# Attention: the outputs' halves turned by transposing DMAs instead of on TensorE, and the fusing products one slot later

## The reference, cut to what matters

```
q    = ln(gelu(x @ Wq @ Wt + bt))                      # 4 groups x 12 heads x 64 = 3072 columns
qf   = concat(relu(q), relu(-q)) / sqrt(128)
out  = (qf @ kv) / (qf @ ksum + 1e-6)                  # per group and head, 64 columns each
h   += gelu(ln(out @ Wf + bf)) @ Wo + bo               # out: [n, 3072], Wf: [3072, 768]
```

## Time and profile before

| | |
|---|---|
| median of 3 runs | 2499.05 us (2498.91 to 2499.41) |
| profiled execution, own time | 2497.05 us |
| its span | 2495.3 us |
| PE, DVE, ACT, POOL busy | 95%, 82%, 74%, 52% of the span |
| mean granted clock of TensorE | 0.984 of full speed |
| attention, about | 706 to 2435 us of the span |
| PE, DVE, ACT, POOL busy of the 200 us from 1200 | 197.5, 161.5, 156.0, 133.2 us |
| idle before the fusing products, on o_lo | 21.7 us, 41 times |
| DMA in attention | none but the loads at its beginning |

### The profile page before, as it was taken

One profiled execution on the slowest core, in us unless ns is written; L12 is line 12 of the kernel. 1 busy time (PEld: TensorE's weight loads), 2 busy tenths in 40 slices (PEclk: granted clock), 3 DMA queues, 4 the chain that ended last, 5 costly groups with the idle time before them and its releaser, 6 DMA issues. The chain is left out here.

```text
span 2495.3 us, 61438 instructions
## 1 busy us (share of the span) xinstructions
PE 2370.7 (95%) x22026; PEld 1669.4 (67%) x22026; DVE 2038.6 (82%) x3219; ACT 1839.3 (74%) x2892; POOL 1292.9 (52%) x1253
## 2 busy tenths in 40 slices
PE   5999999899989999999999999999999999999985
PEld 3777776666656666666666666766666666666654
DVE  7999999878867878787878787878878787878755
ACT  6777777566667777778777878787777778777854
POOL 0000000256666666666666666666666666666660
PEclk9999999999989999999999999999999999999997
DMA  6421111111100000000000000000000000000002
GB/s 142 127 58 38 38 45 31 35 52 44 51 13 2 1 0 0 0 0 0 0 0 0 0 0 0 0 0 0 0 0 0 0 0 0 0 0 0 0 1 64
DMA packets 21800, 46.28 MB, mean 19 GB/s; under 512 B 5684, under 2 KB 12340, under 8 KB 21428
## 3 DMA queue, kind: packets, MB, share of 16 engines
q1 hardware_dynamic: 20596, 45.06, 7.0%
q10 hardware_dynamic: 1152, 0.51, 0.1%
HBM read 41.62 MB, written 3.93 MB: 18 GB/s over the span
## 5 line engine op out<-in xcount | busy, mean ns | idle before, releaser
L1091 ACT ACTIVATE phi<-ps_t,betat,gt 64x512 f32<-64x512 f32 (+1 forms) x1280 | 852.2, 666 | 17.1
L1338 POOL TENSOR_TENSOR phi_lo<-phi 128x512 bf16<-128x512 f32 x480 | 515.4, 1074 | 550.4 <-ACT phi L1091 550.4
L1018 PE MATMUL ps_y<-staging,o_hi 128*128 128x384 bf16 x1920 | 468.7, 326 | 21.7 <-DVE o_lo L1208 21.7
L1018 PE MATMUL ps_y<-staging,o_lo 128*128 128x384 bf16 x1920 | 468.9, 326 | 0.0
L1018 PE MATMUL ps_y<-wf_lo,o_hi 128*128 128x384 bf16 x1920 | 468.9, 326 | 0.0
L1330 POOL TENSOR_TENSOR q_ssq<-q_ssq,half 128x8 f32<-128x8 f32 x240 | 439.2, 1830 | 18.8
L1208 DVE TENSOR_TENSOR o_lo<-ps_u,o_hi 128x512 bf16<-128x512 f32 x240 | 164.4, 685 | 213.9 <-ACT o_hi L1101 213.9
L172 PE MATMUL acc<-w_b,feat 128*128 128x384 bf16 x1728 | 295.5, 331 | 34.2 <-ACT feat L223 28.1
L1101 ACT ACTIVATE o_hi<-ps_u 128x512 bf16<-128x512 f32 x240 | 143.5, 598 | 239.3 <-PE ps_u L1004 239.3
L1018 PEld LDWEIGHTS ps_y<-staging,o_lo 128*128 128x128 bf16 x1920 | 187.9, 98 | 124.2
L1018 PEld LDWEIGHTS ps_y<-wf_lo,o_hi 128*128 128x128 bf16 x1920 | 187.7, 98 | 124.3
(11 more groups left out here) (268 smaller groups left out, 5427.9 us busy)
## 6 DMA issues: line engine op xcount, KB each, us to landing
xt<-in_x_dram SPq DMA_DIRECT2D x32, 320.0 KB, 5.2
ex_big<-in_wf_dram SPq DMA_DIRECT2D x24, 384.0 KB, 3.2
xt<-in_x_dram SPq DMA_DIRECT2D x32, 256.0 KB, 5.7
out_dram<-h SPq DMA_DIRECT2D x8, 480.0 KB, 4.6
staging<-in_wq_t_dram SPq DMA_DIRECT2D x1, 3072.0 KB, 12.6
staging<-in_tok_w_dram SPq DMA_DIRECT2D x8, 240.0 KB, 10.4
staging<-in_tok_w_dram SPq DMA_DIRECT2D x8, 192.0 KB, 10.3
staging<-in_kv_w_dram SPq DMA_DIRECT2D x1, 1536.0 KB, 15.8
```

Source lines behind the costliest of these rows:

```text
L1018: last = nc.tensor.matmul(ps_y[:, n, 0:HC], lhs, w[part][:, c, n * HC:(n + 1) * HC], start=c == 0 and lhs is oh and part == 'wf_hi', stop= ...
L1091: last = nc.scalar.activation(phi[sign * DH:(sign + 1) * DH, j % 2, a:b, head, :], ps_t[rows, a * P:b * P].rearrange("p (i n) -> p i n", n ...
L1338: nc.gpsimd.tensor_tensor(phi_lo[:, j % 2, :, head], phi[:, j % 2, :, head], phi_hi[:, j % 2, :, head], ALU.subtract).then_inc(s["phi_lo_d ...
```

## The change

The halves are now made before the turning. ACT rounds o (in SBUF) into `oh[:, j % 2, 0]`, DVE subtracts into `oh[:, j % 2, 1]`, and SP issues one transposing DMA of the 128 x 1024 bf16 of both into `ot`, with a semaphore for each of the two buffers. PE's `turn_outputs` and the PSUM tile ps_u are gone. `fuse` waits for the DMA and runs in slot k + 3 instead of k + 2. All of the end of a tile moves a slot: `move_y` to slot 3, the root and normalizing to 4, PE's turning and ACT's gelu to 5, `low_ys` and `project_out` to slot 0 of the tile after (the latter still last in PE's slot), `add_to_h` to slot 1, and USES is ordered anew. The last `low_ys` and `project_out` stand behind all slots. In the draining pass GpSimd's `row_roots` stands ahead of `low_ys`. xn, xl and xe move into unused parts of other tiles; one semaphore less is used for the slots' norms.

```diff
-        xn = sb("xn3", [P, 2 * P], F32)
+        xn = flat[:, RING * OC + INNER + OC:]
-        xl = sb("xl3", [P, P], BF16)
-        xe = sb("xe3", [P, P], BF16)
+        xl, xe = (ex['spare'][:, n * P:(n + 1) * P] for n in range(2))
-        o_hi = sb("o_hi", [P, 2, OC], BF16)
-        o_lo = sb("o_lo", [P, 2, OC], BF16)
+        oh = sb("o_halves", [P, 2, 2, OC], BF16)
+        ot = sb("o_turned", [P, 2, 2, PAIRS, P], BF16)
...
-        USES = ("oct3", "oct4", "oct5", "x", "oct0", "oct1", "f0", "f1", "oct2", "r")
+        turned = [sem(f"at_o_turned{n}") for n in range(2)]
+
+        USES = ("oct3", "r", "oct4", "oct5", "x", "oct0", "oct1", "oct2", "f0", "f1")
...
+                def turn_outputs(tile, j):                       # on SP
+                    sp.wait_ge(s["o_lo_done"], count(tile, j, NO))
+                    if (n := earlier(tile, j, NO, 2)) is not None:
+                        sp.wait_ge(s["fused"], n)
+                    sp.dma_start(ot[:, j % 2].rearrange("p k i n -> p (k i) n"),
+                                 oh[:, j % 2].rearrange("p k c -> p (k c)"), transpose=True).then_inc(turned[j % 2], 16)
...
-                def turn_outputs(tile, j):                       # on PE
-                    pe.wait_ge(s["o_done"], count(tile, j, NO))
-                    ...
-                    for i in range(PAIRS):
-                        last = nc.tensor.transpose(ps_u[:, i * P:(i + 1) * P],
-                                                   o[:, i // 2, 2 * (i % 2):2 * (i % 2) + 2].rearrange("p h d -> p (h d)"), ident[:, :])
                 def fuse(tile, j):
-                    pe.wait_ge(s["o_hi_done"], count(tile, j, NO))
-                    pe.wait_ge(s["o_lo_done"], count(tile, j, NO))
+                    pe.wait_ge(turned[j % 2], 16 * count(tile, j // 2, NO // 2))
...
                 def slot(tile, j):                               # on PE
-                    if j == 4 and tile.prev().real:
+                    if j == 5 and tile.prev().real:
                         turn_y(tile.prev(), 0, tile)
...
-                    of, k = octet(tile, j - 2)
+                    of, k = octet(tile, j - 3)
                     if of.real:
                         fuse(of, k)
-                    of, k = octet(tile, j - 1)
-                    if of.real:
-                        turn_outputs(of, k)
-                    if j == 5 and tile.prev().real:
-                        project_out(tile.prev(), tile)
+                    if j == 0 and tile.prev().prev().real:
+                        project_out(tile.prev().prev(), tile)
                 all_slots(pe, slot)
+                project_out(Tile(TILES - 1), Tile(TILES + 1))
...
                 def high_outputs(tile, j):
-                    act.wait_ge(s["o_turned"], count(tile, j, NO))
-                    ...
-                    nc.scalar.activation(o_hi[:, j % 2], ps_u[:, 0:OC], ACT.Copy).then_inc(s["o_hi_done"], 1)
+                    act.wait_ge(s["o_done"], count(tile, j, NO))
+                    if (n := earlier(tile, j // 2, NO // 2, 1)) is not None:
+                        act.wait_ge(turned[j % 2], 16 * n)
+                    nc.scalar.activation(oh[:, j % 2, 0], o[:, :, :, :].rearrange("p a h d -> p (a h d)"),
+                                         ACT.Copy).then_inc(s["o_hi_done"], 1)
...
                 def low_outputs(tile, j):
                     dve.wait_ge(s["o_hi_done"], count(tile, j, NO))
-                    ...
-                    nc.vector.tensor_tensor(o_lo[:, j % 2], ps_u[:, 0:OC], o_hi[:, j % 2],
-                                            ALU.subtract).then_inc(s["o_lo_done"], 1)
+                    nc.vector.tensor_tensor(oh[:, j % 2, 1], o[:, :, :, :].rearrange("p a h d -> p (a h d)"),
+                                            oh[:, j % 2, 0], ALU.subtract).then_inc(s["o_lo_done"], 1)
...
                 def slot(tile, j):                               # on GpSimd
                     if j == 0 and not tile.real and tile.prev().real:
                         row_roots()
-                    if j == 3 and tile.prev().real:
+                    if j == 4 and tile.prev().real:
                         rstd_y(tile.prev())
-                    if j == 5 and tile.prev().real:
-                        low_ys(tile.prev())
+                    if j == 0 and tile.prev().prev().real:
+                        low_ys(tile.prev().prev())
...
                 all_slots(pool, slot)
+                low_ys(Tile(TILES - 1))
```

More of the change, by code:

```diff
@@ L750, in expert_tiles @@
         at += size
+    ex['spare'] = big[:, at:].bitcast(BF16)
     return ex
@@ L899, in read_after @@
                 return tile.next(), [("xe_ready", 0, 1), ("xl_ready", 0, 1)]
-            return tile.prev(), [("h_part", 0, 1)] if use == "r" else [("ys_done", int(use[1:]), 2)]
+            if use == "r":
+                return tile.prev().prev(), [("h_part", 0, 1)]
+            return tile.prev(), [("ys_done", int(use[1:]), 2)]
         def free_bank(eng, tile, use):
@@ L943, in _ @@
                 sp.wait_ge(s["ex_in"], 16 * 20)
+                def turn_outputs(tile, j):
[4 more added lines that the diff above has]
+                                 oh[:, j % 2].rearrange("p k c -> p (k c)"), transpose=True).then_inc(turned[j % 2], 16)
+                for t in range(TILES):
+                    for j in range(NO):
+                        turn_outputs(Tile(t), j)
             @block.tensor
@@ L1014, in fuse @@
                         c = PAIRS * j + i
-                        oh, ol = (v[:, j % 2, i * P:(i + 1) * P] for v in (o_hi, o_lo))
-                        for lhs, part in ((oh, 'wf_hi'), (oh, 'wf_lo'), (ol, 'wf_hi')):
+                        hi, lo = (ot[:, j % 2, k, i, :] for k in range(2))
+                        for lhs, part in ((hi, 'wf_hi'), (hi, 'wf_lo'), (lo, 'wf_hi')):
                             for n in range(2):
                                 last = nc.tensor.matmul(ps_y[:, n, 0:HC], lhs, w[part][:, c, n * HC:(n + 1) * HC],
-                                                        start=c == 0 and lhs is oh and part == 'wf_hi',
-                                                        stop=c == PAIRS * NO - 1 and lhs is ol)
+                                                        start=c == 0 and lhs is hi and part == 'wf_hi',
+                                                        stop=c == PAIRS * NO - 1 and lhs is lo)
                     last.then_inc(s["fused"], 1)
@@ L1205, in low_outputs @@
                     dve.wait_ge(s["o_hi_done"], count(tile, j, NO))
-                    if (n := earlier(tile, j, NO, 2)) is not None:
-                        dve.wait_ge(s["fused"], n)
-                    nc.vector.tensor_tensor(o_lo[:, j % 2], ps_u[:, 0:OC], o_hi[:, j % 2],
-                                            ALU.subtract).then_inc(s["o_lo_done"], 1)
+                    nc.vector.tensor_tensor(oh[:, j % 2, 1], o[:, :, :, :].rearrange("p a h d -> p (a h d)"),
+                                            oh[:, j % 2, 0], ALU.subtract).then_inc(s["o_lo_done"], 1)
                 def move_y(tile):
@@ L1292, in slot @@
                         slots_square()
-                    if j == 4 and not tile.real and prev.real:
+                    if j == 5 and not tile.real and prev.real:
                         dve.wait_ge(s["ex_root"], 3)
-                        row_factors(nc, dve, ex, slice(0, KEPT), s["ex_steps"], 1)
+                        row_factors(nc, dve, ex, slice(0, KEPT), s["ex_steps"], 2)
                         slots_scale()
@@ L1310, in slot @@
                         scale_q(of, k)
-                    if j == 2 and prev.real:
+                    if j == 3 and prev.real:
                         y_stats(prev)
-                    if j == 3 and prev.real:
+                    if j == 4 and prev.real:
                         normalize_y(prev)
```

44 lines of the change are left out of this document (19 added, 25 removed).

## The result

| kernel | time, us (median, range) | ratio to before [95%] | span of the profiled execution |
|---|---|---|---|
| before | 2498.98 (2498.23 to 2499.41) | 1 | 2495.3 |
| changed | 2407.78 (2406.02 to 2408.09) | 0.9634 [0.9617, 0.9651] | 2406.4 |

The change made the kernel 91 us faster; forecast were 2398 us and a range of 2376 to 2500. The profiled executions stand at 2497.05 and 2408.09 us: -89.0, where the sum said -101.1.

The account below looks back on a forecast made before the run. TensorE's issue was taken to bound attention. On the profiled execution, -104.4 - 21.7 + 6 + 12 + 4 + 3 = -101.1 gave 2396 us, and 2398 us for the median of the runs; range 2376 to 2500.

Parts of the forecast that it names:

- the sum: Whole profiled execution: -104.4 - 21.7 + 6 + 12 + 4 + 3 = -101.1 us, so 2396 us.
- The bound: Attention is bound by TensorE's issue; what leaves TensorE counts in full as long as the others keep pace.
- Part 1: The four output transposes of each octet leave TensorE: 40 tiles x 6 octets x 0.435 = 104.4 us removed.
- Part 2: The chain before fusing gets a slot more, so TensorE's 21.7 us wait on the low halves goes.
- Part 3: Shorter attention slots, worst 1 and 4, may stall TensorE: 0 to 48 us, taken as 6 us.
- Part 4: The transposing DMA, one a slot, lands within its cover of 5.8 us at the tightest octet; cost nothing.
- T: Time from the low half's end to the transposing DMA's landing, taken as under 5.8 us.
- Part 5: Start and last pass: +12 us idle behind GpSimd's roots, +4 for the slower clock, +3 for filling at the start.
- (A): Transposed halves land too late for fusing: slower from about 8.6 us on, 2760 us at 10.5; chance 0.20.
- (B): Transposed halves land late, after between 6 and 8.5 us: 2405 to 2495 us; chance 0.10.
- (C): VectorE becomes the bound through slots 3 and 4 and the dearer low half: 2460 to 2495 us; chance 0.07.
- (D): Another wait of 3 us a tile closes the slot, so the change gives nothing: 2495 us; chance 0.03.

Follow-up runs that it names:

- Experiment 4: Kernel before with only fusing and the end of a tile one slot later, outputs still turned by TensorE: 2486.98 us, ratio 0.995.
- experiments 9 and 10: Second part of turning y behind the fusing product: 9 on changed kernel with low halves ahead of roots, 2393.76 us; 10 with y statistics later too, 2399.03 us.
- Experiment 6: Changed kernel with two transposing DMAs an octet, the high and the low half each on its own: 2407.1 us, ratio 0.9637.
- experiment 7: Changed kernel with each octet's halves turned twice, one transfer after the other into the same place: 2411.65 us, ratio 0.9655.
- Experiment 1: Changed kernel with GpSimd's low halves of the gelu ahead of the roots in the last pass: 2392.47 us, ratio 0.9572.
- experiment 8: Changed kernel with each octet's halves turned three times, one transfer after another: 2651.05 us, ratio 1.0613.

## Why the prediction was right, and by how much it was off

**The bound.** Right: what left TensorE counted in full where nothing else was late. Experiment 4 parts the gain: the shift alone gives 12 us, the turning taken away 79.

**Part 1, -104.4.** Right. Plain slots went from 6.58 to 6.14 us.

**Part 2, -21.7.** Right that this wait goes and that what is next late is not the DMA; its size was read too small. The prediction took the idle time before the fusing products, 0.49 us in its tile, for the whole loss and everything else for work. The slot's length says more. Slot 5 of the kernel before:

```profile
1512.09 0.38 PE L955 MATMUL ps_a<-q_hi,xh 128*128 128x512 bf16 x1
...
1520.81 0.38 PE L955 MATMUL ps_a<-q_hi,xh 128*128 128x512 bf16 x1
```

It is 8.72 us, where a plain slot and the projection make 6.58 + 1.49 = 8.07: 0.65 us were lost. The record of the product before the wait lasts 0.2 us, where its successor could have started after 0.03, and so covers a part of the gap. Over the tile, six plain slots, the two turnings (0.22 and 0.65) and the projection make 41.84 us of 42.52: 0.68 us of waiting, 27 us in 40 tiles.

**Part 3, +6.** The right mechanism, and the term that was mis-sized. The working had a tile at 39.4 + 0.15; it is 39.84, so by that base the slots cost 0.42 x 40 = 17 us. The base itself was too high, by part 2's reading: the work of a tile is 6 x 6.14 + 0.22 + 0.65 + 1.49 = 39.20 us, and the 0.64 us above it are all waiting, 26 us. So nearly all of the waiting that went with part 2 came back here. The place was named: slots 4 and 5, behind the bias. VectorE was to enter slot 4 1.6 us late and did so 1.0 us late, and the square waited 1.11 us for it. ScalarE and VectorE in slot 4, which TensorE began at 1495.70:

```profile
1496.68 0.69 DVE L1171 SCALAR_TENSOR_TENSOR shared<-q_sum,shared 128x512 f32<-128x512 f32 x1
...
1497.40 0.63 ACT L1081 ACTIVATE shared<-shared 128x512 f32<-128x512 f32 x1 [1.11 <-DVE shared L1171]
```

The reason given for the small value, that TensorE had shown no such wait before, failed: it was a fact of slots 0.44 us longer, and in experiment 4, whose slots are that long, the excess is absent. The sum looked at the features alone and not at the bank of L1030, whose gelu stands behind the same late square. Nor could the 0.64 us have been won back by moving that product alone: experiments 9 and 10 took 0.36 and 0.82 us out of slot 5, and slot 0 gave them back, since it then hangs on ScalarE's last features of octet 5 and on the sequencer's register work behind them, which no sum of busy times has. The dearer low half (+0.11 us) was rightly priced and harmless; VectorE idles 158 us on the high halves.

**Part 4, the DMA, 0.** Right: T is 3.1 us, 3.0 of it from issue to landing, where the nearest row had 2.6. The Trainium skill, "Advanced Engine Details and Errata", section X-Bar Transpose (TRN2), says that transposing DMAs are as fast as regular ones; the trace agrees, to within 0.4 us for 256 KB. The 1309 ns for a 128 x 128 block in the Trainium skill, "VectorE: DVE Perf Modes", section The three transpose paths, would have been an estimate of 10.5 us for eight blocks one after another. Experiment 6 shows 0.15 us for each block more, so the measurement decides against adding them up. The cover was reckoned as 5.8 us at the tightest octet; experiment 7 gives 6.0.

**Part 5, the ends, +19.** Right: 18 us are left of the total when the tiles' 40 x 2.68 = 107 are taken out. The rows give 11.7 idle (forecast 12.0), 1.4 + 0.5 for the clock (forecast 4; the fusing ran slowly for 1.2 us, not for 4) and 4.1 for the filling, by the first addition of the bias (forecast 3). Experiment 1 confirms the idle time as a loss, and takes it back.

**The sum.** By the lengths of the slots: -104.4 - 27 + 26 + 18 = -87, for -89.0 measured. The forecast said -101.1. Of the 12 us between, part 3 was 20 short; part 2, 5 us too small, and part 5, 1 us too large, hid some of it, and the rest is rounding. That the total came out within 12 us of the forecast owes something to these opposite errors.

**The rivals.** (A) and (B) are out, with T at 3.1 us; experiment 8 shows (A)'s mechanism with its size, and that the sign changes somewhere between T = 6.1 and 9.3 us; where, was not measured. (C) is out: VectorE is busy 86% in attention. (D) is out; the 0.64 us that are left in slot 5 are a small case of it.

The best kernel is that of experiment 1: the change with one order on GpSimd mended, 2392.5 us. Experiment 9, at 2393.8, can't be told from it.

## What to carry to other kernels

Work of the bounding engine that another path can do is worth its full time only if the slot that it shortens has no second chain close behind: check, for every wait of the bounding engine (banks too), how early its releaser is, against the time that the slot loses. Time the waiting by the lengths of the slots: the idle time in the rows of a pipelined engine showed 0.49 of 0.65 us here. Where an order on the bounding engine is changed and the time stays, look for the wait of another engine that its sequencer meets first. A transfer moved off the engine has to be covered by whole slots, and here the later slot was what made the move gain 91 us instead of lose 390. Where a program is drained, look at what long work of a side engine now stands ahead of a short piece that the bound waits for; the order of two calls was worth 15 us.

## What the runs showed of the hardware

A transposing DMA of bf16 between two places in SBUF, 8 blocks of 128 x 128, landed in 3.0 us (3.0 to 4.1 in 240), and 4 blocks in 2.4; SP's issue took 1.23 and 1.19 us, nearly the same for half the blocks. VectorE's operations on two SBUF operands took 0.68 us alone and up to 1.54 beside GpSimd's piece. After 11.7 us idle TensorE ran for 4.0 us at a granted clock of 0.50 to 0.55 and then at 1.00 again. And TensorE's sequencer takes 0.23 to 0.27 us for a head's register operation and instructions, where its products take 0.09: with a lead of 1.5 us at the first of eight the products keep their pace, with 1.1 or 0.7 they fall to the sequencer's. A wait that the sequencer meets ahead of this work sets the lead: it began 0.25 us after ScalarE's last feature.
